# Second cross-attention of a perceiver block: the key stack loaded in two sides, the search for the maxima spread over four groups of chunks

## The reference, cut to what matters

```
Q = (layernorm(x) @ Wq + bq)        # 16 x 64 x 256, 16 heads of 16
K = (layernorm(ctx) @ Wk + bk)      # 16 x 1601 x 256
V = (layernorm(ctx) @ Wv + bv)
A = softmax(Q K^T / sqrt(16))       # over the 1601 rows, for each head
O = A V + Q
out = layernorm(O regrouped) @ Wo + bo + O regrouped
```

## Time and profile before

| | us |
|---|---|
| median of three runs | 1640.6 |
| the profiled execution, its own time | 1641.75 |
| its span, first to last instruction | 1640.0 |
| TensorE busy | 1450.6 (88%) |
| TensorE weight loads busy | 1148.9 (70%) |
| VectorE busy | 995.0 (61%) |
| ScalarE busy | 655.0 (40%) |
| GpSimd busy | 641.6 (39%) |
| mean granted TensorE clock, of 1 | 0.895 |

### The profile page before, as it was taken

One profiled execution on the slowest core, in us unless ns is written; L12 is line 12 of the kernel. 1 busy time (PEld: TensorE's weight loads), 2 busy tenths in 40 slices (PEclk: granted clock), 3 DMA queues, 4 the chain that ended last, 5 costly groups with the idle time before them and its releaser, 6 DMA issues. The chain is left out here.

```text
span 1640.0 us, 29797 instructions
## 1 busy us (share of the span) xinstructions
PE 1450.6 (88%) x11472; PEld 1148.9 (70%) x11472; DVE 995.0 (61%) x1896; ACT 655.0 (40%) x1268; POOL 641.6 (39%) x559
## 2 busy tenths in 40 slices
PE   6988877765994899999999999999999997489998
PEld 3655545444884678888888888888888875357787
DVE  4999964476236556666666666666665652644445
ACT  1444432131200455555545555545555533143322
POOL 0000000001001458777777777787776642222110
PEclk9877788866996899999999999999999985699999
DMA  9479700800142566766657767658666451311000
GB/s 358 157 276 326 266 2 1 298 2 0 59 148 89 139 159 164 188 158 161 158 144 180 173 158 168 150 144 197 169 150 143 98 109 26 107 39 64 0 1 27
DMA packets 109296, 219.61 MB, mean 134 GB/s; under 512 B 10871, under 2 KB 83095, under 8 KB 108391
## 3 DMA queue, kind: packets, MB, share of 16 engines
q1 hardware_dynamic: 109163, 217.80, 47.6%
HBM read 132.51 MB, written 6.40 MB: 85 GB/s over the span
## 5 line engine op out<-in xcount | busy, mean ns | idle before, releaser
L1905 DVE TENSOR_REDUCE d_top<-psum 128x1 f32<-128x400 f32 (+2 forms) x512 | 270.2, 569 | 97.7 <-PE psum L1549 90.5
L1449 POOL TENSOR_TENSOR d_ring<-d_ring 128x512 f32<-128x512 f32 x224 | 290.6, 1297 | 78.8 <-ACT d_ring L1734 61.1
L1734 ACT ACTIVATE d_ring<-psum 128x512 f32<-128x512 f32 (+1 forms) x416 | 229.2, 595 | 207.3 <-PE psum L1567 189.0
L1567 PEld LDWEIGHTS psum<-d_queries,d_stack 100*128 100x128 f32 (+1 forms) x1664 | 214.5, 198 | 36.7 <-issue 34.7
L1567 PE MATMUL psum<-d_queries,d_stack 100*128 100x128 f32 (+1 forms) x1664 | 235.9, 286 | 0.9 <-DVE d_queries L1920 0.9
L1549 PE MATMUL psum<-d_stack,d_queries 96*128 96x400 f32 (+1 forms) x512 | 171.8, 394 | 13.0 <-DVE d_top L1905 10.5
L1379 POOL TENSOR_TENSOR d_rowsT<-d_raw,d_rowsT 128x768 fp32r<-128x768 f32 (+2 forms) x62 | 118.2, 1908 | 156.2 <-ACT d_rowsT L1705 156.2
L1534 PE MATMUL psum<-d_wv,d_rowsT 128*128 128x256 f32 (+1 forms) x1248 | 169.9, 285 | 0.0
L1526 PE MATMUL psum<-d_rowsT,d_wk 128*128 128x384 f32 (+2 forms) x768 | 160.5, 358 | 3.5 <-POOL d_rowsT L1379 1.9
L1534 PEld LDWEIGHTS psum<-d_wv,d_rowsT 128*128 128x128 f32 (+1 forms) x1248 | 161.4, 187 | 0.5 <-issue 0.5
L973 POOL TENSOR_TENSOR c_partL<-moe_in,c_partH 128x256 fp32r<-128x256 f32 x8 | 5.5, 742 | 389.6 <-ACT c_partH L1061 389.6
(11 more groups left out here) (394 smaller groups left out, 2292.6 us busy)
## 6 DMA issues: line engine op xcount, KB each, us to landing
d_stack<-d_stage SPq DMA_DIRECT2D x384, 200.2 KB, 4.2
a_cR<-ctx_rows_dram SPq DMA_DIRECT2D x16, 1664.0 KB, 9.6
a_cT<-ctxT_dram SPq DMA_DIRECT2D x16, 1601.0 KB, 14.4
moe_w<-moe_w_dram SPq DMA_DIRECT2D x16, 1024.0 KB, 10.6
d_rowstd<-row_stds_dram SPq DMA_DIRECT2D x16, 801.0 KB, 5.5
d_raw<-ctxT_dram SPq DMA_DIRECT2D x32, 384.0 KB, 5.7
d_raw<-ctxT_dram SPq DMA_DIRECT2D x16, 512.0 KB, 6.0
d_queries<-queries_dram SPq DMA_DIRECT2D x96, 64.0 KB, 2.0
```

Source lines behind the costliest of these rows:

```text
L1449: pool.tensor_tensor(sums[:, 0, m, :], first, ring[:, slot_of(u, m, c), :], ALU.add)\
L1567: last = pe.matmul(ps[0:w, S_BANK + (m + c) % 2, j * P:(j + 1) * P], stack[0:STACKED, m, j, c * P:c * P + w], queries[0:STACKED, m, j, :], ...
L1734: act.activation(ring[0:w, slot_of(u, m, c), :], ps[0:w, S_BANK + (m + c) % 2, :], ACT.Exp)\
L1905: dve.tensor_reduce(top[:, m, v:v + 1], ps[:, M_BANK + v % 2, 0:min(w, S - s0)], X, ALU.max)\
```

## The change

- `stack` is loaded in two sides of columns: side 0 is chunks 0 to 6 (896 columns), side 1 the other 706. Each side is 12 copies (3584 and 2824 bytes on each of 32 partitions), all on one semaphore; their order takes block j and row range r in turn, so that neighbours have neither source nor destination partitions in common.
- Side 0 of quad n waits for half of the keys (`d_lows`) and for 7 chunks of quad n-2 instead of 13, and is issued from SyncE's queue earlier: for m=0 ahead of the queries, for m=1 between the first two row loads of the batch after next.
- The 16 maxima are found in the order T0 to T7 on side 0 (units 0 and 1 of all four blocks), T8 to T15 on side 1. T0 waits for the whole of side 0, T8 for the whole of side 1.
- They are spread over g1 to g4: 2 at the end of g1 (after `weigh`), then in g2 and g3 two after `score`, two after the fill and one after `weigh`, and four in g4 as before. VectorE's `take_top`s move with them, still at the end of its work for the group.
- `FIRST_TOPS` begins one fill earlier.

```diff
-    TOP_AT = {2: (0, 6), 3: (6, 12), 4: (12, 16)}
+    TOP_AT = {1: ((), (), (0, 1)), 2: ((2, 3), (4, 5), (6,)), 3: ((7, 8), (9, 10), (11,)), 4: ((12, 13), (14, 15), ())}
+    SIDES, SPLIT = 2, 7
+    TOP_ORDER = [(j, 2 * h + i) for h in range(SIDES) for j in range(4) for i in range(2)]
-    FIRST_TOPS = {9: (0, 1), 10: (2, 3), 11: (4, 5, 6, 7), 12: (8, 9, 10, 11), 13: (12, 13), 14: (14, 15)}
+    FIRST_TOPS = {8: (0, 1, 2), 9: (3, 4), 10: (5, 6), 11: (7, 8, 9), 12: (10, 11), 13: (12, 13), 14: (14, 15)}
...
+            def load_side(b, m, h):
+
+                n = 2 * b + m
+                cols = slice(0, SPLIT * P) if h == 0 else slice(SPLIT * P, SE)
+                wait(sp, "d_lows", 4 * n + 2 * h + 2)
+                if n >= 2:
+                    wait(sp, "d_s_ps", NC * (n - 1) if h else NC * (n - 2) + SPLIT)
+                for i in range(12):
+                    j, (part, r) = i % 4, ((0, 0), (1, 32), (0, 64))[i % 3]
+                    sp.dma_start(stack[r:r + 32, m, j, cols].bitcast(F32),
+                                 stage[32 * j:32 * j + 32, m, part, cols].bitcast(F32))\
+                      .then_inc(sig(f"d_stack_in{m}{h}"), 16)
...
                 if now:
-                    load_stack(b, 1)
+                    load_queries(b, 1)
+                    load_side(b, 1, 1)
                     if after:
                         store_own(b + 1, 0)
                 if last_quarter:
                     load_rows(b + 2, 3)
                 if after:
-                    load_stack(b + 1, 0)
+                    load_side(b + 1, 0, 0)
+                    load_queries(b + 1, 0)
+                    load_side(b + 1, 0, 1)
                     store_own(b + 1, 1)
                 if ahead:
                     load_stds(b + 3)
-                    for q in range(3):
+                    load_rows(b + 3, 0)
+                if after:
+                    load_side(b + 1, 1, 0)
+                if ahead:
+                    for q in range(1, 3):
                         load_rows(b + 3, q)
...
-                if v % 4 == 0:
-                    wait(pe, f"d_stack_in{m}{j}", 48 * (b + 1))
+                if v % 8 == 0:
+                    wait(pe, f"d_stack_in{m}{v // 8}", 192 * (b + 1))
...
-                        tops = list(range(*TOP_AT[g])) if ahead and g in TOP_AT else []
+                        tops = TOP_AT[g] if ahead and g in TOP_AT else ((), (), ())
-                        for v in tops[0:2]:
+                        for v in tops[0]:
...
-                        for v in tops[2:4]:
+                        for v in tops[1]:
...
-                        for v in tops[4:6]:
+                        for v in tops[2]:
...
-                            for v in range(*TOP_AT[g]):
+                            for v in sum(TOP_AT[g], ()):
                                 take_top(*nxt, v)
```

More of the change, by code:

```diff
@@ L1289, in load_rows, with load_queries @@
                   .then_inc(sig(f"d_raw_in{q}"), 16)
-            def load_stack(b, m):
+            def load_queries(b, m):
                 n = 2 * b + m
-                wait(sp, "d_lows", 4 * n + 4)
                 wait(sp, "d_s_ps", NC * (n - 1))
@@ L1337, in _ @@
             load_stds(1)
-            for q in range(4):
+            for q in range(2):
                 load_rows(1, q)
-            load_stack(0, 0)
+            load_side(0, 0, 0)
+            for q in range(2, 4):
+                load_rows(1, q)
+            load_queries(0, 0)
+            load_side(0, 0, 1)
             store_own(0, 1)
@@ L1343, in _ @@
               .then_inc(sig("d_marks_in"), 16)
-            load_stack(0, 1)
+            load_side(0, 1, 0)
+            load_queries(0, 1)
+            load_side(0, 1, 1)
             store_own(1, 0)
@@ L1539, in find_top @@
             def find_top(b, m, v):
-                n, j = 2 * b + m, v // 4
-                s0, w = UNITS[v % 4]
+                n, (j, q) = 2 * b + m, TOP_ORDER[v]
+                s0, w = UNITS[q]
                 if v == 0:
@@ L1902, in take_top @@
                 n = 2 * b + m
-                s0, w = UNITS[v % 4]
+                j, q = TOP_ORDER[v]
+                s0, w = UNITS[q]
                 wait(dve, "d_top_ps", TOPS * n + v + 1)
-                dve.tensor_reduce(top[:, m, v:v + 1], ps[:, M_BANK + v % 2, 0:min(w, S - s0)], X, ALU.max)\
+                dve.tensor_reduce(top[:, m, 4 * j + q:4 * j + q + 1], ps[:, M_BANK + v % 2, 0:min(w, S - s0)], X, ALU.max)\
                    .then_inc(sig("d_top"), 1)
```

## The result

| | before | after |
|---|---|---|
| median, us | 1639.86 (4 runs, 1636.55 to 1641.78) | 1656.83 (4 runs, 1651.46 to 1667.88) |
| ratio of the times | | 1.0114, 95% interval 1.006 to 1.0169 |
| profiled execution, its own time | 1641.75 | 1651.46 |
| its span | 1640.0 | 1648.9 |
| mean granted clock | 0.895 | 0.904 |

The change makes the kernel 1.1% slower, 17 us between the medians. The profiled execution after is the quickest of its four and the one before is about the slowest of its four, so that this pair lies only 9.7 us apart.

The account below looks back on a forecast made before the run. The prediction took TensorE to bound the kernel (busy 717.2 of 725 us), its weight loads waiting for VectorE's reductions. Waits 22, clock 10, loads 0 and ends -5 made +27 us, so 1668 us, range 1650 to 1683.

Parts of the forecast that it names:

- Part 1: Maxima spread over g1 to g4: TensorE waits for VectorE ahead of T2, net 0.75 us in 29 quads, +22 us.
- Part 2: TensorE's clock in the quads: half-clock stretches behind the waits, 9 at 3 us less the old 16.6, +10 us.
- 7 new, 2 old: Half-clock falls: 7 at the new wait ahead of T2, 2 of five kept at T14's wait in g4, 3 us each.
- Part 3: Stack copies on SyncE's queue, 24 per quad instead of 12: hidden by at least 4 us, so 0.
- it goes with the bytes: SyncE's queue time per stack copy scales with size: 0.5 us for side 0, 0.4 for side 1, from 0.88.
- Rival D: Stack copies don't get cheaper with size, 0.96 us each; T8 waits 2.2 us in 31 quads: 1736 us, chance 0.06.
- Part 4: Both ends of the layer: first quad 0, stack wait in quad 30 gone -1.3, clock there -4; together -5 us.
- two chances in five: Last quads: chance that the clock holds in the 47 us half-clock stretch, worth 10 us, counted as -4.
- the 0 that I had put there: First quad's maxima (FIRST_TOPS): T2 waits for VectorE in one place instead of later ones; 0, within 1 us.
- Rival A: Kernel gets faster: fewer clock falls behind T14's wait, new stretches too short, end at full clock; -6, 1634 us, chance 0.12.

Follow-up runs that it names:

- e2_spread_only: Kernel before with only the maxima placed as in the change (2, 5, 5, 4 in g1 to g4), old stack and 12 copies: 1661.25 us, ratio 1.0139.
- e4_before_heads_late: Kernel before with VectorE taking the heads of the quad before in g5 instead of g1: 1636.30 us, ratio 0.9989 to the kernel before.
- e9: Kernel after with T2 and T3 behind the fill of g2 and later maxima moved on (2, 3, 5, 6 in g1 to g4): 1626.13 us, 0.9917 to before.
- e10: Kernel after with VectorE's reciprocal of the heads done twice in g1: 1722.79 us, ratio 1.0504 to the kernel before.
- e1: Kernel after, two-sided stack kept, but maxima placed as before the change (6, 6, 4 in g2 to g4): 1635.40 us, ratio 0.9996 to the kernel before.
- e8: Kernel after with each side's 12 copies in the old order, three of one block after another; one execution: 1656.4 us.
- e5: Kernel after with heads in g5 and, in g4 of m=1 quads, T14 and T15 behind weigh: 1616.61 us, ratio 0.9887 to the kernel before.
- e7: As e5, with batch 2's row loads ahead of side 1's copies in the prologue: 1618.85 us, ratio 0.9876 to the kernel before.
- e12: As e11, with the addition of chunk 9 on VectorE instead of GpSimd: 1629.64 us, ratio 0.9951 to the kernel before.
- e6: Kernel before with only T14 and T15 of m=1 quads moved behind weigh in g4: 1623.76 us, ratio 0.9925 to the kernel before.
- e11: Kernel after with maxima placed as before, T14 and T15 of m=1 behind weigh, batch 2's row loads earlier, heads in g1: 1618.76 us, 0.9864 to before.

## Why the prediction was right in sign and some 10 us too high

**Part 1, the waits (+22): right.** VectorE reduces T0 at 2.10 us after the start of `weigh`, as computed (964.41 to 966.51). T2 starts 2.15 us behind T0 (971.71 to 973.86) where 2.15 were expected (964.99 to 967.14). Per quad it came to 0.65 and 0.69 instead of 0.75, +19 us for 28 or 29 quads. `e2_spread_only` and `e4_before_heads_late` show that it is this pairing, tops in g1 behind heads in g1, and nothing else of the change: `e9` keeps both and only moves T2, and the wait is gone; `e10` gives its price at a second size.

**Part 2, the clock (+10): the term that was mis-sized.** In the profiled run it is about 0. The number of falls came out close, with the kinds not as counted: predicted 9 (7 new, 2 old), found 8 between 600 and 1320 us (5 new, 3 old), and a short one at 599 behind the wait of quad 0 for ScalarE. One each of the old and of the new kind, windows of the kernel after:

```profile
677.20:684.00 6.80, 6.80 (x65) 5.17 (x54) 2.87 (x6) 2.89 (x6) 5.69 (x7) 0.50 0.65 182
820.60:823.90 3.30, 3.30 (x25) 2.80 (x27) 1.17 (x3) 0.60 (x1) 3.30 (x4) 0.50 0.85 280
```

and what TensorE did in the second:

```profile
819.49 0.93 PE L1571 MATMUL psum<-d_stack,d_queries 96*128 96x402 f32 x2 [0.67 <-DVE d_top L1928]
820.26 2.54 PE L1556 MATMUL psum<-d_wv,d_rowsT 128*128 128x256 f32 x12
...
824.51 1.01 PE L1589 MATMUL psum<-d_queries,d_stack 100*128 100x128 f32 x8
```

Three falls are of the old kind, in g4 of an m=1 quad, 6.8 us long and 2.9 us dear (971.52 to 998.91 is 27.39 for a quad of 24.47). Five begin behind the new wait and last only 3.4 us: 5.02 us from that T2 to the next scores, against 3.50 in a quad without a fall (973.86 to 977.36), so 1.5 each. 3 x 2.9 + 5 x 1.5 = 16, against 16.6 before. I had given each fall the 3 us of the old ones: Part 2 counted falls and took their length over from another place. Behind the new wait stands at once a fill of 12 matmuls of 256 columns, and the clock is back before it is over; behind the old one stand short matmuls. That this decides the length is not shown: in `e1` the clock fell five times behind the old wait in g4, and two of these falls lasted only 3.4 us (677.3 and 776.3). They began 2.0 us after the start of T14, the three long ones 0.5 to 1.1 us after it.

What stands ahead of each fall in the quads with fills, in every trace, is a wait of TensorE; in `e10` the fall often begins within it. Quad 0 left aside, where the wait is for ScalarE, it is in the kernels before and after, in `e1` to `e4` and in `e8` to `e10` a wait for VectorE among tops and scores: with 0.67 us in g2 five of 29 quads had a fall there (nine in `e2`), with 1.66 us (`e10`) nearly all. It need not be VectorE: `e5`, `e7` and `e12` fell three, two and two times behind the wait for ScalarE in g0, which is 0.8 us in the first two; in the third it is 0.44 or 0.72, right after the 0.42 for the cast. `e6` and `e11` wait 0.5 us there (0.78 once) and did not fall in these quads.

**Part 3, the loads (0): right in the sum, with one term off.** A copy of side 0 takes 0.70 us (8.35 / 12) and one of side 1 0.69 (8.27 / 12), not the 0.5 and 0.4 of "it goes with the bytes"; 24 copies take 16.6 us per quad where 12 took 10.5. The median landing fell from 4.3 to 2.3 us, so the side is complete early enough all the same, and `e1_sides_only` puts the sum at 0 within 0.2%. Rival D (0.96 a copy) would have lost 68 us. A truth between the two, as the text allowed, and the cover was large enough.

**Part 4, the ends (-5): -7.9 in the profiled run, of two parts.** The wait for the stack in quad 30 did not go; it moved from T0 to T8, which waits for side 1. Timeline of TensorE after, to set beside the earlier trace rows:

```profile
1357.79 0.63 PE L1571 MATMUL psum<-d_stack,d_queries 96*128 96x400 f32 x2 [1.42 <-DMA d_stack<-d_stage]
```

1.42 us in place of 1.29. What was gained is the clock: 0.80 from 1320 to 1420 where it was 0.65, the half-clock stretch of 47 us broken up. I had put two chances in five on that, and the trace of `e8`, with one of 41 us, shows that it comes and goes; this part of the forecast came out by luck of the execution as far as these runs tell. At the other end the loop starts 2.6 us earlier (579.12 against 581.74), and TensorE gives 2.0 of it back in quad 0:

```profile
596.92 1.15 PE L1589 MATMUL psum<-d_queries,d_stack 100*128 100x128 f32 x8 [2.00 <-ACT d_ring L1756]
```

The first reciprocal is 0.7 us earlier. Nothing shows that `FIRST_TOPS` brought the earlier start: in the traces with the old one the loop starts between 579.01 (`e1`) and 582.60 (`e2`), with the new one between 579.12 (after) and 584.56 (`e11`). So nothing speaks against the 0 that I had put there.

**The sum.** Forecast +27, measured +17 between the medians and +9.7 in the profiled pair. Its spans differ by 8.9: 18 of waits in 28 quads, -0.6 of clock in them, -8 at the end, -1 at the start. So of the 18 us between this and the forecast the clock in the quads is 10.6, the ends 3.6 and the waits 3.9. An end like that of `e8` explains 7 us more, which is the distance to the medians; but the other three executions after (5 to 16 us above the profiled one) were not traced, so this is the likely reason and not shown. Rival A, the kernel faster because the falls stop, was wrong for this change: three falls stayed at the old wait and five came at the new one. But its mechanism is real and worth 12 us, as `e6` shows.

## What to carry to other kernels

- Before a consumer's input is issued earlier, look at what stands ahead of the consumer in its own queue. Here two reductions were offered 0.95 us sooner (0.57 instead of 1.52 us after the start of `weigh`) to an engine that was bound for 2.1 us, and the producer, with one pair of banks, waited in its place. Put the next dependent piece behind work that needs nobody, as `e9` does, and two tops in g1 cost nothing.
- A short wait of the engine that sets the pace can have two prices: itself, and a half-clock stretch behind it. Here the wait itself was only given back elsewhere, and moving it was still worth 12 us. Where it went with 0.8 us instead of 0.5 (`e5`), some of the falls came back behind it.
- When a wait goes, the pair length tells whether it was gained or moved; the busy time and the count of waits don't.

## What the runs showed of the hardware

- Half-clock stretches of 3.4, 6.8 and 10.2 us made a quad 1.3 to 1.6, 2.5 to 3.1 and 4.6 us longer in these traces, about 0.4 us for each of their microseconds. In the kernel after those behind the wait of g2 are the short ones and those of g4 the longer; what sets the length is open, as `e1` has both behind g4's.
- Halving a copy's bytes in this queue (200 to 112 and 88 KB as the page counts them; 205, 115 and 90 in the prediction are the same) takes its share of the queue from 0.88 us to 0.70 and 0.69 and its landing from 4.2 to 2.3 and 2.2 us, the medians over each kernel.
- One VectorE addition of 128x512 takes 0.68 us with GpSimd idle and 2.15 us in `e12`, where it starts at 972.25 and ends 0.6 us behind GpSimd's product (972.01 to 973.85). The Trainium skill, "SBUF — State Buffer", "Who interferes with whom", says that a VectorE instruction with two inputs in SBUF and a GpSimd instruction that reads SBUF exclude each other for a whole instruction. The rows agree: the 1.47 us over are nearly the 1.60 for which the product still ran. The lone one, in the kernel after:

```profile
968.57 0.68 DVE L1957 TENSOR_TENSOR d_ring<-d_ring 128x512 f32<-128x512 f32 x1
```
